# Two 64-wide attention layers: scores of two heads from 64-row array tiles, in periods of four PSUM banks

## The chip, the core and the metric

The kernel runs on one NeuronCore of a Trainium2 chip. Its engines run side by side and meet only at semaphores: TensorE (PE in the profile; its weight loads are PEld), VectorE (DVE), ScalarE (ACT), GpSimd (POOL) and SyncE (SP), which issues the large DMAs. TensorE writes to PSUM, eight banks of 128 partitions by 512 float32; DVE and ACT read PSUM. The metric is the device time of one execution in microseconds (us). Before the change it is 3609.78 us, the median of 3 runs (3605.16 to 3612.27).

## What is computed

Four layers are applied to 4 batches of 512 tokens of width 256, all in float32. The change touches the attention of the last two layers only, called L2 and L3 here. Cut to what matters:

```python
# L2: 16 heads of 64; one key and value head of 64 shared by all; 512 keys from the context
q = (xn @ Wq).reshape(b, n, 16, 64).transpose(0, 2, 1, 3) * 64 ** -0.5
k, v = kv[..., :64], kv[..., 64:]
attn = softmax(einsum('bhid,bjd->bhij', q, k)); out = einsum('bhij,bjd->bhid', attn, v)
# L3: 16 heads of 64, keys and values per head, 1024 keys (512 of them with a mask)
weight = einsum('bhld,bhnd->bhln', q, k) / 8
weight = softmax(where(full_mask, weight, -FLT_MAX)); out = einsum('bhln,bhnd->bhld', weight, v)
```

## The kernel before

The program is one instruction stream per engine with hand-placed semaphore waits. It goes through layer 0 attention, an expert layer, layer 1, and from about 1430 us through L2 and L3 once per batch: L2 of batch 0 alone, then a loop over three passes that each do L3 of batch b and L2 of batch b+1, then L3 of the last batch.

Both attentions come from one helper, `attention`, called as `att2` and `att3`. Its unit is a step: one head and 128 of the 512 queries. Two heads make a group, which has 4 query tiles x 2 heads = 8 steps; there are 8 groups, so 64 steps per call. `banks` is the number of PSUM banks that the scores of a step fill: 1 in L2 (512 keys), 2 in L3 (1024 keys). A step goes through these stations:

- `score` (L221, PE): one 512-column matmul per bank. The contraction is 64 long, but it is done over all 128 rows: the queries of both heads lie in `qT`, and each head has its own key tile `kH[..][s]` whose other 64 rows hold zeros. A float32 matmul is two passes of the array, two rows of the profile.
- `find` (DVE): the row minimum of the negated scores, L275 in L2; in L3 the mask is added in the same instruction, L277.
- `exponent` (L316, ACT): the exponential from PSUM to `probs` (the tile `pbuf`) with the row sum.
- `invert` and `divide` (L283 and L288, DVE): the reciprocal of the sum, and the probabilities times it.
- `turn` (L233, PE): four 128x128 transposes per bank into PSUM bank 4 or 5, in turns.
- `keep_turned` (L326, ACT): the copy of that bank to SBUF (`work`).
- `values` (L243, PE), once per group: probabilities times values, the two heads in the two 64-column halves of the array; `keep_values` (L292, DVE) copies the result.

Scores have banks 0 to 3 as a ring: `ring` = 4 steps in L2 and 2 in L3. PE runs ahead by that many steps, and DVE divides `behind` = 2 or 1 steps after it finds. PE's order in a step is `score(n + ring)`, `turn(n)`, and then at most a few jobs. Jobs are pieces of other work laid between the steps: the projections of the next group (L2: queries, L1692; L3: queries L1692, keys twice L1896, values twice L1904, each four 512-column or sixteen 128-column passes), and in the loop the normalisation of the next batch (during L3) or the last linear layer (during L2). PE makes a job's product in bank 7 and waits for DVE's copy of the one before (`jobs_kept`).

## Time and profile before

| what | us |
|---|---|
| median of 3 runs | 3609.78 |
| span of the profiled execution | 3697.7 |
| L2 attention, batch 0 alone | 128.20 |
| L2 attention in the loop, three calls | 131.98, 131.97, 131.98 |
| L3 attention in the loop, three calls | 297.11, 297.11, 297.13 |
| L3 attention, last batch alone | 289.85 |
| one pass of the loop (L2's last `values` of one to that of the next) | 554.99 |

The profiled execution has no time of its own beside its span, which is 88 us longer than the median of the runs. The eight attention calls, each counted from its first score matmul to the first matmul behind it, make up 1705 us of the span. Busy time is the sum of an engine's instructions; the end of a matmul is modelled, and consecutive ones overlap by their latency, so the distance between the starts of two matmuls tells what PE really needs for the first.

### The profile page before, as it was taken

Reading aid. Unit: us, or ns where it says so; the run is one execution under the profiler, and the core shown is the slowest. Engines: PE = TensorE matmul, PEld = TensorE weight load, DVE = VectorE, ACT = ScalarE, POOL = GpSimd, SP = SyncE. Lnnn points to the kernel's source line nnn. Section 1 sums busy time; section 2 is a strip of 40 time slices with the busy share of each in tenths; the row PEclk is TensorE's granted clock in tenths of the full one; section 3 lists DMA queues with packets and bytes.
Section 4 is the critical chain, followed back from the end, with each engine's and each line's share of the span. In section 5 each row is a group of like instructions: output and inputs, shape, how many; then the busy total and the mean of one; then the engine's idle time right before and its main releaser. Section 6 shows DMA issues by size and latency. Waiting matters only on the chain. (4 is left out here: it accounts for less than half of the span.)

```text
span 3697.7 us, 39640 instructions
## 1 busy us (share of the span) xinstructions
PE 3091.5 (84%) x13360; PEld 1710.1 (46%) x13360; DVE 2076.9 (56%) x5810; ACT 1450.9 (39%) x3056; POOL 384.7 (10%) x458
## 2 busy tenths in 40 slices
PE   7887877456077576998999988999988999988997
PEld 3443434222035254554555454555454555454554
DVE  6675756411357576634665734665734665734655
ACT  5463635221022221623444623444623444623443
POOL 0021202142652440000000000000000000000000
PEclk9998989678577777999999999999999999999998
DMA  1000000188562532001001001001001001001000
GB/s 47 15 13 15 12 15 12 60 252 243 101 83 29 85 46 86 1 3 67 1 1 46 1 19 57 1 1 46 1 18 58 1 1 46 1 19 45 1 1 6
DMA packets 47720, 143.61 MB, mean 39 GB/s; under 512 B 13735, under 2 KB 21287, under 8 KB 43563
## 3 DMA queue, kind: packets, MB, share of 16 engines
q1 hardware_dynamic: 32682, 111.82, 9.0%
q0 software_dynamic: 14848, 29.45, 5.9%
q8 instruction: 97, 1.59, 0.2%
q14 instruction: 93, 0.75, 0.1%
HBM read 128.43 MB, written 12.80 MB: 38 GB/s over the span
## 5 line engine op out<-in xcount | busy, mean ns | idle before, releaser
L221 PE MATMUL ps<-kH,qT 128*128 128x512 f32 x2048 | 1016.6, 601 | 26.3 <-issue 10.4
L326 ACT ACTIVATE work<-ps 128x512 f32<-128x512 f32 x768 | 430.3, 596 | 735.7 <-PE ps L233 466.7
L277 DVE CUSTOM_DVE_ANT_0 ps<-ps,mask 128x1024 f32<-128x1024 f32 x256 | 314.9, 1230 | 363.0 <-PE ps L221 361.1
L316 ACT ACTIVATE pbuf<-ps,least 128x512 f32<-128x512 f32 (+1 forms) x512 | 460.7, 900 | 132.6 <-DVE least L275 112.8
L233 PEld LDWEIGHTS ps<-consts,pbuf 128*128 128x128 f32 x3072 | 363.3, 141 | 279.6 <-issue 181.8
L221 PEld LDWEIGHTS ps<-kH,qT 128*128 128x128 f32 x2048 | 339.6, 192 | 269.0 <-issue 244.2
L233 PE MATMUL ps<-consts,pbuf 128*128 128x128 f32 x3072 | 421.1, 273 | 10.9 <-DVE pbuf L288 10.9
L243 PE MATMUL ps<-work,vh 128*64 128x512 f32 x1536 | 343.7, 596 | 5.7 <-ACT work L326 5.7
L288 DVE TENSOR_SCALAR pbuf<-pbuf,recip 128x512 f32<-128x512 f32 (+1 forms) x512 | 315.0, 615 | 10.9
L326 ACT ACTIVATE pt<-ps 128x512 f32<-128x512 f32 x256 | 152.4, 597 | 175.1 <-remote 84.6
L233 PEld LDWEIGHTS ps<-consts,probs 128*128 128x128 f32 x1024 | 124.6, 143 | 192.5 <-issue 106.9
L1233 POOL DMA_INDIRECT yg<-expert_rows,idx x192 | 201.0, 1047 | 91.5 <-issue 53.8
L243 PEld LDWEIGHTS ps<-work,vh 128*64 128x64 f32 x1536 | 104.5, 137 | 226.5 <-issue 218.9
L233 PE MATMUL ps<-consts,probs 128*128 128x128 f32 x1024 | 162.1, 281 | 40.6 <-issue 21.4
L489 POOL DMA_INDIRECT slot_token<-token_i,place x128 | 125.1, 977 | 639.3 <-DVE token_f L805 531.4
L316 ACT ACTIVATE probs<-ps,least 128x512 f32<-128x512 f32 x256 | 175.0, 683 | 37.8 <-DVE least L277 36.8
L277 DVE CUSTOM_DVE_ANT_0 ps<-ps,mask_add 128x512 f32<-128x512 f32 x256 | 174.3, 681 | 19.7 <-remote 11.6
L275 DVE TENSOR_REDUCE least<-ps 128x1 f32<-128x512 f32 x256 | 172.7, 675 | 13.1 <-PE ps L221 12.8
L283 DVE RECIPROCAL recip<-sums 128x1 f32<-128x1 f32 x768 | 121.8, 159 | 84.2 <-ACT probs L316 29.1
L1896 PE MATMUL ps<-arena 128*128 128x512 f32 x256 | 127.7, 623 | 27.2 <-ACT arena L1972 27.2
L1332 PE MATMUL ps<-ctxT,gw 128*36 128x512 f32 x32 | 23.0, 885 | 136.7 <-DMA ctxT<-in_ctxT 136.7
L1904 PE MATMUL ps<-arena 128*128 128x128 f32 x1024 | 127.6, 279 | 0.0
(288 smaller groups left out, 3645.6 us busy)
## 6 DMA issues: line engine op xcount, KB each, us to landing
wgu<-in_L_wgu SPq DMA_DIRECT2D x32, 768.0 KB
wd<-in_L_wd SPq DMA_DIRECT2D x32, 384.0 KB
arena<-in_L_wo SPq DMA_DIRECT2D x8, 1024.0 KB, 10.3
arena<-in_L_wff SPq DMA_DIRECT2D x4, 2048.0 KB, 9.4
ctxT<-in_ctxT SPq DMA_DIRECT2D x8, 512.0 KB, 3.7
expert_rows<-y SPq DMA_DIRECT2D x32, 128.0 KB
xb<-x_scratch SPq DMA_DIRECT2D x8, 512.0 KB, 3.5
ctxb<-in_ctx SPq DMA_DIRECT2D x8, 512.0 KB, 4.7
```

What stands on the lines that cost most here:

```text
L221: last = nc.tensor.matmul(scores(n)[:, kb * BANK:(kb + 1) * BANK], q_of(g, s, qt), k_of(g, s, kb), start=True, stop=True)
L233: last = nc.tensor.transpose(ps[:, 4 + m % 2, c * P:(c + 1) * P], probs[n % np_][:, kc * P:(kc + 1) * P], ident)
L243: last = nc.tensor.matmul(ps[rows * s:rows * (s + 1), 6, :], v_of(g, s, kc), pts[g % len(pts)][:, s, kc, :], start=kc == 0, stop=kc == nk - 1)
L275: nc.vector.tensor_reduce(least[:, n % 8:n % 8 + 1], x, AX.X, ALU.min).then_inc(least_ready, 1)
L277: nc.vector.tensor_tensor_reduce(out=x, in0=x, in1=mask, scale=1.0, scalar=FMAX, op0=add, op1=ALU.min, accum_out=least[:, n % 8:n % 8 + 1])\
L288: nc.vector.tensor_scalar(p, p, recip[:, n % 8:n % 8 + 1], None, mult).then_inc(probs_ready, 1)
L316: nc.scalar.activation(probs[n % np_], scores(n), ACT.Exp, bias=least[:, n % 8:n % 8 + 1], scale=-1.0, accum_out=sums[:, n % 8:n % 8 + 1]) ...
L326: nc.scalar.activation(pts[g % len(pts)][:, s, kb * 4:kb * 4 + 4, qt * P:(qt + 1) * P], ps[:, 4 + m % 2, :].rearrange("p (c q) -> p c q", ...
L489: nc.gpsimd.indirect_dma_start(taken_d[:, :], bass.IndirectOffsetOnAxis(place8[:, t, k:k + 1], 0), token_i[:, t:t + 1], None, bounds_check ...
L1233: nc.gpsimd.indirect_dma_start(yg[j % 2][:, k, :], None, y_d[:, :], bass.IndirectOffsetOnAxis(idx8s[u][:, t * TOPK + k:t * TOPK + k + 1], ...
L1896: last = nc.tensor.matmul(ps[:, bank, :], wkx[:, c, g * P:(g + 1) * P], keysT[:, c, kb * BANK:(kb + 1) * BANK], start=c == 0, stop=c == DC ...
L1904: last = nc.tensor.matmul(ps[:, bank, i * P:(i + 1) * P], keysT[:, c, tok], wvx[:, c, g * P:(g + 1) * P], start=c == 0, stop=c == DC - 1)
```

## The change

L2 and L3 use a new helper, `attention_pairs`; layer 0 keeps `attention`.

- Scores: the two heads of a group are two matmuls with a contraction of 64, one from rows 0 to 63 of `qT` and `kH`, one from rows 64 to 127. `kH` is one tile per buffer without zeros, and its copies (L1706 and L1915 in the helper jobs, L1935 for the first group) are one instruction, not two.
- The unit is a period: four score banks, which is U = 4 steps in L2 and 2 in L3. PE scores a whole period ahead, and only once all exponentials of the period before have been read from those four banks.
- `turn` goes in two halves of two banks each. Half 0 is copied to SBUF by DVE, half 1 by ACT. Both halves use banks 4 and 5, so half 1 waits for DVE's copies, and half 0 of the next period for ACT's.
- DVE makes one reciprocal per half; GpSimd makes the divisions.
- Jobs keep their step numbers, but are placed behind the half in which their step lies; DVE does its part at the end of a period.

```diff
--- before.py
+++ after.py
+def attention_pairs(nc, sem, name, ps, ident, groups, banks, q_of, k_of, v_of, mask, bufs, out, jobs):
...
+    U = 4 // banks
+    HALF = U // 2
+    nk = 4 * banks
+    per = 2 * NT
+    N = groups * per // U
+    each_group = per // U
+    probs, sums, recip, least, pts = bufs
...
+    def where(n):
+        g, r = divmod(n, per)
+        return g, r // 2, r % 2
...
+    def turned_at(p, half, j):
+        n = p * U + half * HALF + (j if banks == 1 else 0)
+        return n, (0 if banks == 1 else j)
+    def turned_to(p, half, j):
+        n, kb = turned_at(p, half, j)
+        g, qt, s = where(n)
+        return pts[g % len(pts)][:, s, kb * 4:kb * 4 + 4, qt * P:(qt + 1) * P]
+    def turned_from(j):
...
+        def score(p):
+            g = p // each_group
+            if p % each_group == 0 and need[g]:
+                pe.wait_ge(jobs_kept, need[g])
+            if p:
+                pe.wait_ge(exp_ready, p * U)
+            if banks == 1:
+                for n in range(p * U, (p + 1) * U):
+                    g, qt, s = where(n)
+                    nc.tensor.matmul(scores(n), q_of(g, s, qt), k_of(g, s, 0), start=True, stop=True).then_inc(scores_ready, 1)
+                return
+            for kb in range(banks):
+                for n in range(p * U, (p + 1) * U):
+                    g, qt, s = where(n)
+                    last = nc.tensor.matmul(scores(n)[:, kb * BANK:(kb + 1) * BANK], q_of(g, s, qt), k_of(g, s, kb),
+                                            start=True, stop=True)
+                    if kb == banks - 1:
+                        last.then_inc(scores_ready, 1)
+        def turn(p, half):
+            for j in range(2):
+                n, kb = turned_at(p, half, j)
+                if j == 0 or banks == 1:
+                    pe.wait_ge(probs_ready, n + 1)
+                if half:
+                    pe.wait_ge(kept_v, 2 * p + j + 1)
+                elif p:
+                    pe.wait_ge(kept_a, 2 * (p - 1) + j + 1)
+                for c in range(4):
+                    kc = kb * 4 + c
+                    last = nc.tensor.transpose(ps[:, 4 + j, c * P:(c + 1) * P], probs[n % np_][:, kc * P:(kc + 1) * P], ident)
+                last.then_inc(turned, 1)
+        def values(g):
+            pe.wait_ge(kept_v, 2 * each_group * (g + 1))
+            pe.wait_ge(kept_a, 2 * each_group * (g + 1))
+            if g:
+                pe.wait_ge(av_kept, g)
+            for kc in range(nk):
+                for s in range(2):
+                    last = nc.tensor.matmul(ps[64 * s:64 * (s + 1), 6, :], v_of(g, s, kc), pts[g % len(pts)][:, s, kc, :],
+                                            start=kc == 0, stop=kc == nk - 1)
+            last.then_inc(av_ready, 1)
+        score(0)
+        for p in range(N):
+            if p + 1 < N:
+                score(p + 1)
+            if p and p % each_group == 0:
+                values(p // each_group - 1)
+            for half, jobs_here in enumerate(halves(p, before)):
+                turn(p, half)
+                for job in jobs_here:
+                    project(job)
+        values(groups - 1)
...
+        def invert(p, half):
+            n = p * U + half * HALF
+            v.wait_ge(exp_ready, n + HALF)
+            at = slice(n % 8, n % 8 + HALF)
+            nc.vector.reciprocal(recip[:, at], sums[:, at]).then_inc(recip_ready, 1)
+        def keep_turned(p, j):
+            g = p // each_group
+            if p % each_group == 0 and g >= len(pts):
+                v.wait_ge(av_ready, g - len(pts) + 1)
+            v.wait_ge(turned, 4 * p + j + 1)
+            nc.vector.tensor_copy(turned_to(p, 0, j), turned_from(j)).then_inc(kept_v, 1)
+        def keep_values(g):
+            v.wait_ge(av_ready, g + 1)
+            nc.vector.tensor_copy(out[:, g, :], ps[:, 6, :]).then_inc(av_kept, 1)
+        for n in range(U):
+            find(n)
+        invert(0, 0)
+        invert(0, 1)
+        for p in range(N):
+            if p + 1 < N:
+                for n in range((p + 1) * U, (p + 2) * U):
+                    find(n)
+            if p and p % each_group == 0:
+                keep_values(p // each_group - 1)
+            for j in range(2):
+                keep_turned(p, j)
+                if p + 1 < N:
+                    invert(p + 1, j)
+            for jobs_here in halves(p, before):
+                for job in jobs_here:
+                    keep_job(job)
+        keep_values(groups - 1)
...
+        def exponent(n):
+            act.wait_ge(least_ready, n + 1)
+            if n >= np_:
+                act.wait_ge(turned, (n - np_ + 1) * banks)
+            nc.scalar.activation(probs[n % np_], scores(n), ACT.Exp, bias=least[:, n % 8:n % 8 + 1],
+                                 scale=-1.0, accum_out=sums[:, n % 8:n % 8 + 1]).then_inc(exp_ready, 1)
+        def keep_turned(p, j):
+            g = p // each_group
+            if p % each_group == 0 and g >= len(pts):
+                act.wait_ge(av_ready, g - len(pts) + 1)
+            act.wait_ge(turned, 4 * p + 2 + j + 1)
+            nc.scalar.activation(turned_to(p, 1, j), turned_from(j), ACT.Copy).then_inc(kept_a, 1)
+        for n in range(U):
+            exponent(n)
+        for p in range(N):
+            if p + 1 < N:
+                for n in range((p + 1) * U, (p + 2) * U):
+                    exponent(n)
+            for j in range(2):
+                keep_turned(p, j)
+    def divide(pool):
+        for n in range(groups * per):
+            pool.wait_ge(recip_ready, n // HALF + 1)
+            x = probs[n % np_]
+            nc.gpsimd.tensor_scalar(x, x, recip[:, n % 8:n % 8 + 1], None, mult).then_inc(probs_ready, 1)
...
-        kH = [[keep(f"kH_{i}{s}", [P, KEYS3]) for s in range(2)] for i in range(2)]
+        kH = [keep(f"kH_{i}", [P, KEYS3]) for i in range(2)]
...
-            def copy(v):
-                for s in range(2):
-                    r = slice(64 * s, 64 * s + 64)
-                    last = nc.vector.tensor_copy(kH[0][s][r, 0:S], ps[r, 7, :])
-                return last
-
-            return product, copy
+            return product, lambda v: nc.vector.tensor_copy(kH[0][:, 0:S], ps[:, 7, :])
...
-        att2 = attention(nc, sem, "a2", ps, ident, 2, HP, NT,
-                         lambda g, s, qt: qT[g % 2][:, qt * P:(qt + 1) * P],
-                         lambda g, s, kb: kH[0][s][:, 0:S],
-                         lambda g, s, kc: vh[0][:, kc, 0:DH2], DH2, None,
+        def head(s):
+            return slice(64 * s, 64 * s + 64)
+        att2 = attention_pairs(nc, sem, "a2", ps, ident, HP, 1,
+                         lambda g, s, qt: qT[g % 2][head(s), qt * P:(qt + 1) * P],
+                         lambda g, s, kb: kH[0][head(s), 0:S],
+                         lambda g, s, kc: vh[0][:, kc, 0:DH2], None,
...
-        att3 = attention(nc, sem, "a3", ps, ident, 2, HP, KEYS3 // P,
-                         lambda g, s, qt: qT[g % 2][:, qt * P:(qt + 1) * P],
-                         lambda g, s, kb: kH[g % 2][s][:, kb * BANK:(kb + 1) * BANK],
-                         lambda g, s, kc: vh[g % 2][:, kc, s * DH2:(s + 1) * DH2], DH2, mask3[:, :],
+        att3 = attention_pairs(nc, sem, "a3", ps, ident, HP, 2,
+                         lambda g, s, qt: qT[g % 2][head(s), qt * P:(qt + 1) * P],
+                         lambda g, s, kb: kH[g % 2][head(s), kb * BANK:(kb + 1) * BANK],
+                         lambda g, s, kc: vh[g % 2][:, kc, s * DH2:(s + 1) * DH2], mask3[:, :],
...
-                for i in range(2):
-                    nc.vector.memset(kH[i][0][64:P, :], 0.0)
-                    link(nc.vector.memset(kH[i][1][0:64, :], 0.0))
...
+            @block.gpsimd
+            def _(pool):
+                att3[6](pool)
+                att2[6](pool)
```

## Rows read from the trace of the kernel before

**Rows 1.** The page: the clock granted to PE, in 40 slices, in tenths.

```profile
PEclk9998989678577777999999999999999999999998
```

**Rows 2.** Windows: length, busy (instructions) of PE, PEld, DVE, ACT, POOL; clock; DMA.

```profile
1473.68:1601.88 128.20, 126.19 (x541) 62.76 (x541) 82.62 (x206) 82.27 (x193) 0.00 (x0) 1.00 0.00 1
3129.54:3261.52 131.98, 128.51 (x557) 64.14 (x557) 95.27 (x252) 82.38 (x193) 0.00 (x0) 1.00 0.09 37
3370.07:3659.92 289.85, 285.54 (x1333) 159.69 (x1333) 171.28 (x313) 141.57 (x257) 0.00 (x0) 1.00 0.00 1
```

**Rows 3.** Timeline of one L2 step: start, length in us, engine, line, operation.

```profile
3202.17 1.02 PE L221 MATMUL ps<-kH,qT 128*128 128x512 f32 x2
3202.45 0.67 DVE L275 TENSOR_REDUCE least<-ps 128x1 f32<-128x512 f32 x1
3203.04 0.48 DVE L288 TENSOR_SCALAR pbuf<-pbuf,recip 128x512 f32<-128x512 f32 x1
3203.46 1.02 PE L221 MATMUL ps<-kH,qT 128*128 128x512 f32 x2
```

**Rows 4.** Timeline around the values of two L2 groups, two groups apart.

```profile
3180.01 3.65 PE L243 MATMUL ps<-work,vh 128*64 128x512 f32 x16
...
3211.76 3.65 PE L243 MATMUL ps<-work,vh 128*64 128x512 f32 x16
...
3215.35 1.12 PE L221 MATMUL ps<-kH,qT 128*128 128x512 f32 x2
...
3216.51 0.69 DVE L275 TENSOR_REDUCE least<-ps 128x1 f32<-128x512 f32 x1 [0.28 <-PE ps L221]
```

**Rows 5.** Chain of waits through an L3 group: start us, us, what.

```profile
3401.96 1.72 PE ps L221 x4
3404.55 1.72 PE ps L221 x4
3406.27 0.87 PE ps L233 x8
...
3408.86 7.02 PE ps L243 x32
3415.88 1.91 PE ps L221 x4
...
3427.28 1.79 PE ps L1904 x16
...
3445.54 7.02 PE ps L243 x32
```

**Rows 6.** Timeline at the start of an L3 call, before the pipeline is full.

```profile
3373.56 1.11 ACT L316 ACTIVATE pbuf<-ps,least 128x1024 f32<-128x1024 f32 x1 [2.24 <-DVE least L277]
...
3374.82 1.98 PE L221 MATMUL ps<-kH,qT 128*128 128x512 f32 x4 [1.05 <-ACT pbuf L316]
...
3376.84 1.23 DVE L277 CUSTOM_DVE_ANT_0 ps<-ps,mask 128x1024 f32<-128x1024 f32 x1 [0.93 <-PE ps L221]
```

**Rows 7.** Timeline: a DVE copy of a PSUM bank and the instruction behind it.

```profile
3458.52 0.69 DVE L292 COPY wide<-ps 128x512 f32<-128x512 f32 x1
...
3459.13 1.22 DVE L277 CUSTOM_DVE_ANT_0 ps<-ps,mask 128x1024 f32<-128x1024 f32 x1
```

**Rows 8.** Groups of GpSimd instructions: busy, mean ns of one, idle before.

```profile
L1297 POOL TENSOR_SCALAR_AFFINE_SELECT eT<-eT 128x128 f32<-128x128 f32 x64 | 18.5, 307 | 34.7 <-ACT eT L1449 34.1
L971 POOL COPY column<-taken 128x1 uint32 x28 | 5.2, 184 | 46.7 <-PE ps L992 46.7
```

**Rows 9.** Timeline of PE in the expert layer, and of PE ahead of an L3 call.

```profile
857.67 1.51 PE L1001 MATMUL ps<-wgu,xgT 128*64 128x384 f32 x8 [0.47 <-DMA wgu<-in_L_wgu]
860.52 0.42 PE L1009 MATMUL ps<-consts,h 128*96 128x128 f32 x2 [1.34 <-DVE h L1100]
...
862.75 2.83 PE L1001 MATMUL ps<-wgu,xgT 128*64 128x384 f32 x8 [0.43 <-DMA wgu<-in_L_wgu]
...
3354.91 3.78 PE L1896 MATMUL ps<-arena 128*128 128x512 f32 x4 [5.46 <-ACT arena L1972]
```

More of the change, by code:

```diff
@@ L1912, in keys @@
             def keys(kb):
-                def copy(v):
-                    for s in range(2):
-                        r = slice(64 * s, 64 * s + 64)
-                        last = nc.vector.tensor_copy(kH[g % 2][s][r, kb * BANK:(kb + 1) * BANK], ps[r, 7, :])
-                    return last
-                return lambda pe: key_product(g, kb, 7), copy
+                return (lambda pe: key_product(g, kb, 7),
+                        lambda v: nc.vector.tensor_copy(kH[g % 2][:, kb * BANK:(kb + 1) * BANK], ps[:, 7, :]))
             def vals(kb):
@@ L1933, in keep_first @@
             if kind == "keys":
-                for s in range(2):
-                    r = slice(64 * s, 64 * s + 64)
-                    last = nc.scalar.activation(kH[0][s][r, kb * BANK:(kb + 1) * BANK], ps[r, bank, :], ACT.Copy)
-                return last
+                return nc.scalar.activation(kH[0][:, kb * BANK:(kb + 1) * BANK], ps[:, bank, :], ACT.Copy)
             if kind == "values":
@@ L2139, in _ @@
                 r2_vector(v)
+            @block.gpsimd
+            def _(pool):
+                att3[6](pool)
+                att2[6](pool)
         link.n = 0
@@ L2161, in _ @@
                 rest[1](v)
+            @block.gpsimd
+            def _(pool):
+                att3[6](pool)
 def kernel(**inputs):
```

60 lines of the change are left out of this document (added).

## Prediction

> **What bounds the kernel now.** The windows over the eight attention calls come first. PE is busy 126.2 of 128.2 us in L2 alone, 128.5 of 132.0 in L2 of the loop and 285.5 of 289.9 in L3, with the full clock; DVE is busy 59 to 72% of them, ACT 49 to 64%, GpSimd not at all [rows 2]. The timeline of a step then shows why. In L2 one step follows the next by 1.29 us [rows 3]: two score passes and four transposes. The chain of waits through an L3 group is all PE [rows 5]: four score passes take 1.72 us (0.43 each), eight transposes 0.87, together the 2.59 us between two steps. A group takes 31.75 / 2 = 15.88 us in L2 [rows 4] and 36.68 in L3 [rows 5]. So a cheaper score matmul is on the path, but only until something else is later.
>
> **Scores in pairs.** Of the 0.43 us per pass, half should go if two 64-row passes run at once. The nearest row is the value product, where two heads share the array by columns: 32 passes take 7.02 us, so 16 pairs at 0.43 and 0.14 over, and the next scores take 1.91 where 1.72 is usual [rows 5]. A pair thus costs as much as one pass, and going into such a mode and out again about 0.33. No row shows pairs by rows, so a pair costs between 0.43 (side by side) and 0.86 (one behind the other). I take 0.43, the row of the same array split the other way. Per L2 group 16 passes become 8 pairs, per L3 group 32 become 16: 3.4 and 6.9 us less PE work, over 4 x 8 groups of each 330 us. Off that go mode changes, some 0.2 us for each of the new ones. The Trainium skill, "TensorEngine Tiling (Array Packing)", section Tiling Modes, says that different tiles can compute in parallel, and that a change of mode drains the engine. The overhead of the value rows agrees with the second.
>
> **The period's loop.** Here the gain is lost. Before, PE was two or four steps ahead in a ring. Now the four banks are one buffer, and there is a second loop through banks 4 and 5. In iteration p PE issues `score(p+1)`, half 0, half 1. Half 1 waits for `kept_v`, DVE's copies of half 0, and these are queued on DVE behind all finds of p+1, which wait for the scores just issued. Only then can PE go on to `score(p+2)`. Counted from a period's first score:
>
> - L3: the finds can start at 2.02 (scores at 3374.82, L277 at 3376.84) [rows 6]. Two finds of 1.23 [rows 6] end at 4.48. Two copies of a bank: one starts 0.61 after the other and lasts 0.69 [rows 7], so 1.30. Then 0.05 for a semaphore, 0.10 for a weight load that is not hidden, 0.43 for four transposes and 0.10 to leave the mode: 2.02 + 2.46 + 1.30 + 0.68 = 6.46 us for two steps, which were 5.19. The exponentials are earlier: the second starts about 0.1 behind its find, and PE is free 1.26 after its start [rows 6], at 5.8.
> - L2: the finds start at 1.16 (L221 at 3215.35, L275 at 3216.51) [rows 4], four of 0.59 (start to start in [rows 3]): 1.16 + 2.36 + 1.30 + 0.68 = 5.50 us for four steps, which were 5.18.
>
> PE alone would need 1.72 + 1.74 + 0.3 = 3.8 us of either period. Only periods with the value product or with jobs are filled by PE.
>
> **Group by group.** L2 has two periods. The first holds scores 1.72, values 3.44, transposes 1.74, the query job 1.72 and four changes of mode at 0.15: 9.2. The second is the loop, 5.5. Sum 14.7, against 15.88. L3 has four. The first: scores 1.72, values 6.88, transposes 1.74, two jobs 3.44, changes 0.6: 14.4. In the second one job hides in half 0, but the value job in half 1 waits for DVE's copy of the one before, at 6.7, and adds 1.79 [rows 5]: 8.5. Third and fourth are loops, the one job hidden: 2 x 6.46. Sum 35.8, against 36.68. With 32 groups of each: -38 and -28 us. At the ends: a call begins with one period that nothing covers (5.2 us in L2, 5.9 in L3, where the ring needed 4 to 5), and its last group has no jobs to fill PE. Laid out per call, L2 is 5.2 + 2 x 5.5 + 6 x 14.7 + 15.4 = 119.8 against 128.2 [rows 2], and L3 is 5.9 + 29.9 + 6 x 35.8 + 36.0 = 286.6 against 289.85 [rows 2]. In the loop L3 has 7.3 us of normalisation jobs; some 3 of them hide in idle half 0. Sum: -4 x 8.4 - 4 x 3.3 - 3 x 3 = -56 us.
>
> **The clock.** PE was hardly idle in these calls, and the clock stayed full. In the fourth L3 period it now works some 3.4 of 6.46 us, with a pause of about 2.4 in one piece. The expert layer shows what that can do: there PE pauses 1.34 us behind 1.51 us of L1001, and the next eight of L1001 take 2.83 [rows 9], that is 1.2 GHz and not 2.4; the page has slices of 0.6 to 0.8 there [rows 1]. Behind a pause of 5.46 us four passes take 3.78 [rows 9] against 1.72. I expect one fall in two groups of three of L3, none in L2 (its longest pause is 1.5 us), and price it at 1.6 us, since the transposes and scores behind it, 2 us at full clock, nearly double: 32 x 2/3 x 1.6 = 34. Each of the eight calls also begins with a pause of 3 to 4 us: 8 x 1.5 = 12. Sum +46. Its bounds are 0 and, with two falls in every L3 group, +115. The Trainium skill, "TensorE: Matmul & The Clock Gate", section on the clock gate, has the same two levels and says that idling throttles the array; the rows of the expert layer agree.
>
> **GpSimd.** 256 divisions of 128x512 and 256 of 128x1024 leave DVE. The nearest rows are an instruction on 128x128 at 307 ns and a copy of one column at 184 [rows 8]. A 128x1024 one is then between 0.184 + 8 x 0.123 = 1.2 us and 8 x 0.307 = 2.5; I take 1.7, between them, since the fixed part is seen but not the rate of this operation. The reciprocal of half 0 is ready at about 5.2 of the period, and its transposes come at 6.46 + 2.0; half 1 has until 11.6 for both. So up to about 3.2 us each is hidden by PE's own scores, and GpSimd adds nothing to the sum. The Trainium skill, "GPSIMD Engine Reference", section 3.1, gives 1.8 cycles per element at 1.2 GHz at best, 1.5 us here, also hidden. No run here shows it.
>
> **Small edits.** One key copy where there were two takes some 0.7 us [rows 7] per L3 key job off DVE, each behind a PE product that is later; four memsets lie under the first loads. Both nothing, at most -5.
>
> **Sum.** -56 + 46 = -10 us against the profiled execution, 3697.7 to 3688. The 88 us between it and the median are not located; I carry the difference over unchanged: 3610 - 10 = 3600.
>
> **Rivals.** (A) The forecast, 3600, its own range 3580 to 3620. (B) The clock holds, because the pauses are split by transposes: -56, 3554. For it: the longest pause is half that ahead of L3. Against: the expert layer falls behind a shorter one. (C) The loop is longer than its rows: waits that no row shows, at PE's two waits or at DVE's copies, or further falls. Some 112 periods are bound by the loop (32 in L2, 80 in L3); at 0.5 us each +56, so 3656, slower. It decides from 0.1 us each. For it: every station now waits for another one in turn, and each hop is shown only once. (D) The change does not do what it says: row pairs run one behind the other. Each period's scores take 1.72 us more, at the head of the loop: 4 x 32 + 4 x 16 = 192 periods, +330 less the clock loss that then goes: about 3880. For it: two 128-column results go to PSUM at once, which no row shows. GpSimd above 3.2 us, for which no row speaks, would look like C.
>
> **Chances.** A 0.42, B 0.27, C 0.23, D 0.08. A measurement of this kernel tells 0.2% (7 us) from no change. Of A half lies below 3603, a quarter within. Faster: B and most of half of A, 0.49; same: 0.12; slower: C, D and the rest of A, 0.39. The range leaves out D and the ends of B and C: 3535 to 3680.
>
> **What would show it.** Right: in L2 and L3 the score passes start in pairs, 0.43 apart; in L3 periods without values or jobs PE waits some 2.4 us for DVE's `keep_turned`, and the period is 6.4 to 6.6 us; DVE's copies sit directly behind the finds; GpSimd ends before PE asks. Groups of 14.7 and 35.8 us plus the clock. The granted clock below 1 in L3 only. Wrong: PE waiting for GpSimd or for ACT's exponentials at the head of a period, score passes 0.86 apart, or groups over 16 and 37.5 us at full clock.

## The result and the profile after

The changed kernel takes 3658.19 us (median of 4 runs, 3655.99 to 3659.97), the kernel before in the same visit 3607.47 us: ratio 1.0144, 95% interval 1.0130 to 1.0159. It is 51 us slower. The forecast was 3600, 10 us faster. The time lies inside the range, near rival C (3656), but that is luck: C's main mechanism, longer loops, is not what the trace shows. The ratios here and below leave out one execution of run e12, the profiled one, which ran at a lower granted clock throughout (4136.77 us, the others 3604.68 to 3621.44).

Windows over three of the eight attention calls, the changed kernel (L2 alone, L2 in the loop, L3 last; columns as in [rows 2], which they answer):

```profile
1374.84:1503.76 128.92, 112.03 (x541) 53.71 (x541) 71.35 (x142) 64.44 (x161) 98.84 (x64) 0.94 0.00 1
...
3065.61:3202.65 137.04, 116.84 (x556) 56.73 (x557) 88.86 (x188) 64.39 (x161) 100.12 (x64) 0.93 0.09 35
...
3310.50:3616.97 306.47, 270.09 (x1332) 139.78 (x1332) 151.41 (x299) 115.14 (x193) 181.18 (x64) 0.93 0.00 1
```

PE has 14 us less busy time in L2 alone and the call is 0.7 us longer; in the last L3 call 15 us less busy time and 16.6 us longer. The clock, the third figure from the right, is the news: 0.93 and 0.94 where every call of before had 1.00.

The measure used below, "the calls", is a sum of five spans that hold the eight calls: L2 alone, three stretches of the loop from L3's first score pass to the end of L2's last value product, and the last L3 call. Each stretch also holds 15.5 us of other work between its two calls, the same in every kernel, so the sum stands 46.6 us above the eight calls by themselves (1702.4 before, 1756.4 after); the expectations call it the sum of the eight calls. It is 1749.0 us before and 1803.0 after: +54.0, which is the whole difference. (The rest of the program took 1852 us in the profile of after, and 1947 to 1958 or 1851 to 1859 in the profiles further down, by the visit and not by the kernel. The profile of before had 1949 there; that is where its surplus over the median lies. So absolute times are not compared across visits, ratios and the calls are.)

PE's timeline through a steady L3 group (start, length in us; L428 scores, L454 values, L444 transposes, L1912, L2113 and L2121 jobs), which answers [rows 5]:

```profile
3430.73 3.17 PE L454 MATMUL ps<-work,vh 128*64 128x512 f32 x14
...
3439.35 1.99 PE L428 MATMUL ps<-kH,qT 64*128 64x512 f32 x8
...
3447.90 1.99 PE L428 MATMUL ps<-kH,qT 64*128 64x512 f32 x8
...
3454.47 1.99 PE L428 MATMUL ps<-kH,qT 64*128 64x512 f32 x8 [0.16 <-DVE vh L2135]
3456.39 1.09 PE L444 MATMUL ps<-consts,pbuf 128*128 128x128 f32 x8
3459.64 1.23 PE L444 MATMUL ps<-consts,pbuf 128*128 128x128 f32 x8 [2.17 <-DVE work L503]
3460.80 3.28 PE L428 MATMUL ps<-kH,qT 64*128 64x512 f32 x8
3464.01 7.44 PE L454 MATMUL ps<-work,vh 128*64 128x512 f32 x32
```

To see here: eight passes of 64 rows take 1.99 us, the time of four of 128 rows, so they do run in pairs. The periods are 8.55, 6.57 and 6.33 us. In the last one PE stands 2.17 us before half 1, for DVE's copy of half 0 (L503). Right behind that pause the same eight passes take 3.28 us instead of 1.99, and the value product that follows 7.44 where 7.09 is usual. In the L3 calls of the loop the fall comes a little earlier: the value product is at 7.09, but the transposes before the scores take 1.5 to 1.7 us instead of 1.23, and the scores 3.0 to 3.3. Each of the six steady groups of each L3 call has one stretch at half clock, 24 in all, and the kernel before has none in any call; steady groups are 37.4 to 37.65 us, against 36.68 before. The window over these scores alone:

```profile
3460.80:3464.01 3.21, 3.21 (x10) 0.96 (x9) 0.00 (x0) 0.70 (x2) 3.21 (x2) 0.59 0.02 5
```

The end of the last L3 call, PE's and GpSimd's rows. There is no next score to cover anything:

```profile
3591.96 1.23 PE L444 MATMUL ps<-consts,pbuf 128*128 128x128 f32 x8 [2.17 <-DVE work L503]
3593.12 1.99 PE L428 MATMUL ps<-kH,qT 64*128 64x512 f32 x8
...
3598.32 5.66 POOL L556 TENSOR_SCALAR pbuf<-pbuf,recip 128x1024 f32<-128x1024 f32 x2 [0.67 <-DVE recip L496]
...
3601.21 1.93 PE L444 MATMUL ps<-consts,pbuf 128*128 128x128 f32 x8 [1.69 <-POOL pbuf L556]
...
3604.03 1.97 PE L444 MATMUL ps<-consts,pbuf 128*128 128x128 f32 x8 [0.89 <-POOL pbuf L556]
...
3606.73 9.46 PE L454 MATMUL ps<-work,vh 128*64 128x512 f32 x32 [0.73 <-issue]
```

The two divisions take 2.83 us each, PE waits for both, and the last value product takes 9.46 us where 7.09 is its full-clock time. The first two rows hold a warning: here a pause of 2.17 us stands before the transposes too, and the scores behind it keep 1.99 us; so do those of the first group in two of the loop's L3 calls. So the length of one pause does not decide by itself whether the clock falls. L2's call ends in the same way, on four divisions of 1.55 us:

```profile
1493.38 0.66 PE L444 MATMUL ps<-consts,pbuf 128*128 128x128 f32 x4 [0.88 <-POOL pbuf L556]
...
1494.92 0.81 PE L444 MATMUL ps<-consts,pbuf 128*128 128x128 f32 x4 [0.88 <-POOL pbuf L556]
...
1498.30 5.52 PE L454 MATMUL ps<-work,vh 128*64 128x512 f32 x16 [0.73 <-issue]
```

GpSimd by form (busy us, mean ns | idle before), which answers the guess made from [rows 8]:

```profile
L556 POOL TENSOR_SCALAR pbuf<-pbuf,recip 128x1024 f32<-128x1024 f32 x256 | 725.0, 2843 | 922.1 <-DVE recip L496 922.1
L556 POOL TENSOR_SCALAR pbuf<-pbuf,recip 128x512 f32<-128x512 f32 x256 | 399.2, 1576 | 301.9 <-DVE recip L496 301.9
```

### The profile page after: what moved, and what is told of

It is laid out like the page before. It is cut to its first block and busy times, and to the rows that moved or that the text cites. A ratio compares the mean times of both kernels' runs of the same rounds, so it can differ in the third digit from the quotient of the medians.

```text
span 3654.7 us, 39585 instructions
## 1 busy us (share of the span) xinstructions
PE 2921.7 (80%) x13360; PEld 1587.1 (43%) x13360; DVE 1978.3 (54%) x5490; ACT 1264.3 (35%) x2664; POOL 1509.7 (41%) x970
## 5 line engine op out<-in xcount | busy, mean ns | idle before, releaser
L556 POOL TENSOR_SCALAR pbuf<-pbuf,recip 128x512 f32<-128x512 f32 (+1 forms) x512 | 1124.1, 2210 | 1224.0 <-DVE recip L496 1224.0
L444 PE MATMUL ps<-consts,pbuf 128*128 128x128 f32 x3072 | 456.4, 288 | 161.6 <-DVE work L503 144.2
L444 PEld LDWEIGHTS ps<-consts,pbuf 128*128 128x128 f32 x3072 | 342.8, 144 | 412.1 <-POOL pbuf L556 200.4
L454 PE MATMUL ps<-work,vh 128*64 128x512 f32 x1536 | 358.9, 618 | 6.0 <-issue 6.0
L541 ACT ACTIVATE work<-ps 128x512 f32<-128x512 f32 x384 | 223.4, 596 | 379.9 <-PE ps L444 368.9
L428 PE MATMUL ps<-kH,qT 64*128 64x512 f32 x1024 | 290.9, 692 | 23.0 <-ACT pbuf L533 15.8
L221 PE MATMUL ps<-kH,qT 128*128 128x512 f32 x512 | 261.8, 598 | 6.3 <-DVE qT L908 5.6
L503 DVE COPY work<-ps 128x512 f32<-128x512 f32 x384 | 258.2, 679 | 8.5 <-PE ps L444 8.4
L454 PEld LDWEIGHTS ps<-work,vh 128*64 128x64 f32 x1536 | 110.4, 142 | 253.0 <-issue 253.0
L507 DVE COPY wide<-ps 128x512 f32<-128x512 f32 x64 | 44.3, 692 | 262.2 <-PE ps L454 262.2
L428 PEld LDWEIGHTS ps<-kH,qT 64*128 64x128 f32 x1024 | 100.9, 212 | 141.8 <-issue 104.6
L2113 PE MATMUL ps<-arena 128*128 128x512 f32 x256 | 131.0, 636 | 28.2 <-ACT arena L2181 27.5
```

The costliest lines, as they stand in the source:

```text
L221: last = nc.tensor.matmul(scores(n)[:, kb * BANK:(kb + 1) * BANK], q_of(g, s, qt), k_of(g, s, kb), start=True, stop=True)
L428: last = nc.tensor.matmul(scores(n)[:, kb * BANK:(kb + 1) * BANK], q_of(g, s, qt), k_of(g, s, kb), start=True, stop=True)
L444: last = nc.tensor.transpose(ps[:, 4 + j, c * P:(c + 1) * P], probs[n % np_][:, kc * P:(kc + 1) * P], ident)
L454: last = nc.tensor.matmul(ps[64 * s:64 * (s + 1), 6, :], v_of(g, s, kc), pts[g % len(pts)][:, s, kc, :], start=kc == 0, stop=kc == nk - 1)
L503: nc.vector.tensor_copy(turned_to(p, 0, j), turned_from(j)).then_inc(kept_v, 1)
L541: nc.scalar.activation(turned_to(p, 1, j), turned_from(j), ACT.Copy).then_inc(kept_a, 1)
```

## The experiments

Three theories are tried. K: the half clock behind PE's pauses is the loss. G: GpSimd's slow divisions are, where nothing covers them. L: the chain of waits through the four banks is, whatever the clock does. Every run is compared with the kernel before in the same visit.

| kernel | ratio to before (95%) | the calls, us | steady group L3 / L2 |
|---|---|---|---|
| before | 1 | 1749.0 | 36.7 / 15.88 |
| changed | 1.0144 (1.0130 to 1.0159) | 1803.0 | 37.5 / 14.72 |
| e1 | 1.0074 (1.0057 to 1.0091) | 1777.3 | 36.8 / 15.51 |
| e2 | 1.0283 (1.0265 to 1.0302) | 1846.5 | 36.8 / 15.51 |
| e3 | 1.0183 (1.0162 to 1.0204) | 1814.6 | 37.5 / 15 to 16.5 |
| e4 | 1.0552 (1.0534 to 1.0569) | 1946.4 | 40.4 / 17.0 |
| e5 | 0.9955 (0.9939 to 0.9971) | 1744.2 | 35.9 / 14.72 |
| e6 | 0.9879 (0.9853 to 0.9904) | 1702.7 | 33.8 / 14.72 |
| e7 | 0.9795 (0.9774 to 0.9816) | 1664.3 | 33.8 / 13.94 |
| e8 | 0.9741 (0.9721 to 0.9762) | 1651.5 | 33.8 / 13.95 |
| e9 | 0.9731 (0.9700 to 0.9763) | 1659.5 | 33.8 / 13.95 |
| e10 | 0.9707 (0.9682 to 0.9733) | 1645.1 | 33.8 / 13.95 |
| e11 | 1.0323 (1.0298 to 1.0347) | 1868.8 | 38.2 / 16.74 |
| e12 | 1.0023 (1.0008 to 1.0037) | not read | not read |

### e1, e2, e5 and e12: more work in the pause

If the clock is the cause, giving PE something useless to do in the pause must make the kernel faster.

```
         for half, jobs_here in enumerate(halves(p, before)):
             turn(p, half)
+            if half == 0 and not any(job[0] is not None for job in jobs_here):
+                fill(4 if banks == 2 else 3)
...
+        def fill(times, bank=7):
+            if bank == 7 and done[0]:
+                pe.wait_ge(jobs_kept, done[0])
+            for _ in range(times):
+                nc.tensor.matmul(ps[:, bank, :], ident, spare, start=True, stop=True)
```

> The changed kernel, plus matmuls whose result nobody reads: wherever half 0 of a period has no job, PE writes bank 7 four times (L3) or three times (L2) before it asks for the copies that half 1 waits for. Theory K (the half clock behind PE's pause of 2.17 us is the loss): the scores behind a jobless L3 period go back from 3.28 to 1.99 us and the value products from 7.45 to 7.09, so a steady L3 group falls from 37.55 to 35.8 us. About 30 such groups: -50 us, 3608, ratio to the kernel before 0.997 to 1.003, although PE does more. L2 groups stay at 14.7. Theory G (GpSimd's 2.83 us per division, waited for at starts and ends of calls) and theory L (the chain of waits itself, whatever the clock): the groups stay at 37.5, 3655 to 3665, since the added matmuls hide in the pause at best.

Measured: ratio 1.0074, calls 1777.3, half of what K expected. L3 groups fell to 36.82 and L2 groups rose to 15.51. The trace shows that the fault is in the dose. A matmul of this kind is two passes of 0.43 us, not one, so four of them take 3.44 us in a pause of 2.17 (L462 is the fill):

```profile
3526.10 1.99 PE L428 MATMUL ps<-kH,qT 64*128 64x512 f32 x8 [0.16 <-DVE vh L2143]
...
3528.95 3.60 PE L462 MATMUL ps<-consts 128*128 128x512 f32 x8
3532.39 1.04 PE L444 MATMUL ps<-consts,pbuf 128*128 128x128 f32 x8
3533.35 1.99 PE L428 MATMUL ps<-kH,qT 64*128 64x512 f32 x8
3535.27 7.09 PE L454 MATMUL ps<-work,vh 128*64 128x512 f32 x32
```

The scores behind it are back at 1.99 and the values at 7.09: the clock held, and the period, 7.25 us, is now filled by PE's own work. The second run had the same fault in more places.

```
         score(0)
+        fill(8, 6)
...
+                if p == N - 1:
+                    fill(2 if half else 4)
                 turn(p, half)
...
+        fill(2)
         values(groups - 1)
```

> As the one before, and also eight unread matmuls behind the first scores of each call (bank 6), and 4, 2 and 2 of them ahead of the last three waits of each call (two halves of the last period, last value product). Theory K: the second scores of a call fall from 3.78 to 1.99, the last value product from 9.46 to 7.1 (L3) and from 5.52 to 3.65 (L2): some 4 us in each of 8 calls more than the run before, -80 us in all, 3575 to 3585, ratio 0.99 to 0.993: faster than the kernel before. Theory G: the waits for GpSimd at the ends stay, and nothing is gained but what the first run gained. Rival within K: matmuls ahead of a wait that is short (0.7 us) make PE late themselves, +0.5 us per call.

Measured: 1846.5. The steady groups are those of e1. The first scores of the last L3 call lie 8.99 us before the second, which were 5.93 apart, and from the last but one value product to the last it takes 38.9 us where it took 30.09 in the changed kernel. This is twice the intended work, in places without cover, and as a forecast of the time the expectation is a miss. What it says of the clock came true: in seven of the eight calls no stretch is at half clock, the second scores take 1.99 us, and the last value products 7.09 and 3.65. The clock was kept, at a price above what it is worth.

So the dose was fitted, with the changed kernel as the base again:

```
+                    fill(2 if banks == 2 else 1)
```

> As the first run (unread matmuls in jobless half 0), but two of them (1.72 us) in L3 and one (0.86 us) in L2, so that they fit into pauses of 2.17 and 1.38 us; the first run's four and three took 3.44 and 2.58 and made the periods longer (7.25 where 6.34). The measure is the sum of the eight attention calls (first score to end of last value product), since the layers ahead take 1850 or 1950 us from one visit to the other: 1749.0 in the kernel before, 1803.0 in the changed one, 1777.3 in the first run. Theory K: steady L3 group 35.9 us (predicted working without a clock loss: 35.8), L2 14.7, calls 1725 to 1735: faster than the kernel before by 15 to 25 us, ratio 0.993 to 0.997. Rival: two matmuls leave 0.45 us of pause and PE's clock falls all the same, 37.0 to 37.5 per group, 1790 to 1803.

Measured: 0.9955 (0.9939 to 0.9971), calls 1744.2, L3 group 35.90, L2 group 14.72. A group of the last L3 call:

```profile
3501.93 1.99 PE L428 MATMUL ps<-kH,qT 64*128 64x512 f32 x8 [0.16 <-DVE vh L2143]
3503.85 1.09 PE L444 MATMUL ps<-consts,pbuf 128*128 128x128 f32 x8
3504.78 1.88 PE L462 MATMUL ps<-consts 128*128 128x512 f32 x4
3507.11 1.22 PE L444 MATMUL ps<-consts,pbuf 128*128 128x128 f32 x8 [0.45 <-DVE work L511]
3508.26 1.99 PE L428 MATMUL ps<-kH,qT 64*128 64x512 f32 x8
3510.18 7.09 PE L454 MATMUL ps<-work,vh 128*64 128x512 f32 x32
```

The period is still 6.33 us, the loop of waits untouched, with 1.72 us more work in it. Yet the group is 1.6 us shorter, 1.3 in the scores and 0.35 in the values. No steady L3 group has a stretch at half clock any more. That is K, by itself 1803.0 - 1744.2 = 59 us, more than the whole slowdown; 41 of it lie in the L3 calls and 18 in L2's, whose first and sixth groups in the loop and last value products had lost the clock too. L and G expected no change. (The profiled execution took 10 us more than the median of its kernel, so 59 is rather low than high; the ratio stands for 16 us under the kernel before.)

e5 does not hold the clock everywhere. Its last L3 call, from which the group above is taken, is at 0.98:

```profile
3362.89:3656.99 294.10, 274.50 (x1377) 143.95 (x1377) 151.43 (x299) 114.97 (x193) 181.39 (x64) 0.98 0.00 1
```

```
+                    fill(1 if banks == 2 else 0)
```

> The changed kernel with one unread matmul (0.86 us) in the jobless half 0 of L3, none in L2: half of what filled the pause before. The pause of 2.17 us is then 1.3 in one piece. Theory K in its simple form (a pause of that length costs nothing: L2's steady groups have one of 1.38 and stay at full clock): L3 group 35.9 as with two. Rival: what counts is how much PE works around the pause, not its length, and it still falls once a group: 37.0 to 37.5. L2 as in the changed kernel. Calls 1750 to 1760 by the first, 1790 to 1803 by the second.

Measured: 1.0023 (1.0008 to 1.0037), that is 7 us over the kernel before, so calls of about 1756. No group is read from its trace. The total fits the first reading, 1750 to 1760: in L3 half the dose does nearly all of it. That is shown by the total alone.

### e3 and e9: where the division is done

```
+        def split(p, half):
+            v.wait_ge(recip_ready, 2 * p + half + 1)
+            for n in range(p * U + half * HALF, p * U + (half + 1) * HALF):
+                x = probs[n % np_]
+                nc.vector.tensor_scalar(x, x, recip[:, n % 8:n % 8 + 1], None, mult).then_inc(probs_ready, 1)
...
             for job in jobs_here:
                 keep_job(job)
+            if p + 1 < N:
+                split(p + 1, half)
```

> The changed kernel with the divisions of a half on DVE, behind its copies and the jobs of that half, and nothing on GpSimd. Theory G: at the end of a call PE waits 2.6 us (L3) and 3.7 us (L2) for GpSimd, and in L2's start another 0.8 to 1.2 per period; with DVE's 0.5 to 0.9 us per division most of that goes, so 2 to 4 us per call, -15 to -30 us, 3628 to 3643, with steady groups as they were (14.7 and 37.5). Theory K: the same small gain at the ends, since the clock is not touched. Rival: DVE now has finds 2.46, copies 1.30, divisions 1.8 and reciprocals 0.3 in a period of 6.34, and a job's copy on top makes it the bound: L3 periods with one job grow by 0.2 to 0.5, 0 to +30 us in all.

Measured: 1.0183, calls 1814.6, 12 us more than the changed kernel, where 15 to 30 less were expected. G is right on two places. In L2 alone the way from the last but one value product to the end of the last falls from 18.8 to 14.0 us. The last L3 call is 6.7 us shorter (299.0 from its first score, was 305.7): 4.2 at its end, with the last value product at 7.09, and 2.5 at its start, where this run lost less to the clock (second scores 2.53 us, were 3.78). In the three L3 calls of the loop nothing is gained at the end, 38.6 us where 38.5 was: there the products for the next L2 call lie between the last transposes. The steady L3 group stays at 37.54, so GpSimd was hidden there. The rival showed in L2 and not in L3, where I had put it. On DVE a division of 128x1024 takes 0.744 us; L2 in the loop has DVE busy 111.2 of 144.1 us with it (88.9 of 137.0 without; the window below stops 2.8 us short, in the last value product). Its groups go from 15 to 17 and 19 us, and it has five stretches at half clock in its middle where the changed kernel has two:

```profile
3177.19:3318.50 141.31, 116.18 (x544) 58.49 (x546) 111.22 (x252) 64.18 (x161) 0.00 (x0) 0.90 0.09 34
```

So the division is better on DVE at the end of L3 and on GpSimd in L2's steady groups. The run e9 prices that in the version e8 below, by taking back only this edit:

> The version of the last run with L3's divisions on GpSimd again: it parts that run's two edits. Calls were 1664.3 with the jobs spread and 1651.5 with unread matmuls and DVE's divisions on top. Theory G: at the end of an L3 call PE waits for GpSimd (1.69 and 0.89 us in the changed kernel), so this one is 2 to 4 us longer per L3 call than the last: 1660 to 1668, and the unread matmuls alone bring little. Theory K: what was gained is the clock at the ends, brought by the unread matmuls: 1651 to 1655.

Measured: calls 1659.5, 8 us over e8, as G expected, but not for G's reason in each call. In the last L3 call it is: the way from the last but one value product to the last is 29.76 us with GpSimd and 28.09 without. The L3 calls of the loop are 0.4, 2.6 and 2.5 us longer; there 2.3 us more in the last group is also what e5 and e6, both with GpSimd, show in one of their three calls and not in the others, with the clock down in it. So 1.7 us is shown for GpSimd, and the rest of the 8 is open. The ratios, 0.9731 and 0.9741 in two visits, can't tell the two apart.

### e4 and e11: what the pairs are worth

```
-        kH = [keep(f"kH_{i}", [P, KEYS3]) for i in range(2)]
+        kH = [[keep(f"kH_{i}{s}", [P, KEYS3]) for s in range(2)] for i in range(2)]
...
-                         lambda g, s, qt: qT[g % 2][head(s), qt * P:(qt + 1) * P],
-                         lambda g, s, kb: kH[g % 2][head(s), kb * BANK:(kb + 1) * BANK],
+                         lambda g, s, qt: qT[g % 2][:, qt * P:(qt + 1) * P],
+                         lambda g, s, kb: kH[g % 2][s][:, kb * BANK:(kb + 1) * BANK],
```

> The changed kernel with keys padded to 128 rows, as in the kernel before, so that no two score passes run at once; periods, copies and GpSimd stay. If pairs save what the rows say, an L2 period issues 1.72 us of passes where it had 0.86 x 2 ... that is 4 x 0.43 against 2 x 0.43, and L3 3.44 against 1.72. L2 group: the period bound by PE grows by 0.86, the loop does not: 15.6 us. L3 group: first period 14.4 + 1.7, second +1.4, two loops 7.7 each where they were 6.4: about 41.5 plus the clock's loss, which stays (PE still pauses 2.6 us for DVE's copies). Sum +0.9 x 32 + 4.5 x 32 = +170 us, 3800 to 3850, ratio 1.05 to 1.07. If pairs do not run at once, no change: 3658. That gives the price of the periods alone against the kernel before.

Measured: 1.0552, calls 1946.4. Without pairs the same structure is 143 us slower than with them; against the kernel before, the periods (with GpSimd's division) cost 197 us. The L3 group, 40.4, is near what was expected (41.5), but the clock's loss, which was to stay, is gone: no L3 call has a stretch at half clock between its first and its last but one value product. The pause is 1.47 us where 2.17 was, and 3.44 us of scores stand around it where 1.72 did. So the 143 us are the pairs' saving less what they cost in clock. The L2 group, 17.0, is not (15.6): I had counted one pass where a score has two, so that both periods pay 1.72 us or some less:

```profile
1541.54 3.70 PE L423 MATMUL ps<-kH,qT 128*128 128x512 f32 x8
1545.07 1.04 PE L444 MATMUL ps<-consts,pbuf 128*128 128x128 f32 x8
1546.71 1.28 PE L444 MATMUL ps<-consts,pbuf 128*128 128x128 f32 x8 [0.60 <-DVE work L503]
1547.83 3.60 PE L423 MATMUL ps<-kH,qT 128*128 128x512 f32 x8
```

The fourth period of an L3 group, with the shorter pause and the scores behind it at full speed:

```profile
3653.05 1.22 PE L444 MATMUL ps<-consts,pbuf 128*128 128x128 f32 x8 [1.47 <-DVE work L503]
3654.11 3.60 PE L428 MATMUL ps<-kH,qT 128*128 128x512 f32 x8
```

e11 is the same edit on e8:

> The best version with padded keys, so that no two score passes run at once: what do the pairs bring where jobs are spread and the clock holds? Rows of the fourth run: scores take 3.44 us of a period, not 1.72. L2 group: 13.95 + 2 x 1.72 = 17.4, less what of the loop PE then hides. L3 group: first period +1.72, three loop periods: second half's copies end at 3.0 + 2.46 + 1.3 = 6.8, +0.7 = 7.5 where 6.4 is, together 33.75 + 1.7 + 3.3 = 38.8. Calls: 1651 + 32 x 3.0 + 32 x 5.0 = about 1900, ratio 1.03 to 1.05 to the kernel before: the pairs carry the whole gain. Rival: the order of jobs and the held clock carry it, and pairs are worth less than half of the 98 us: 1750 or less.

Measured: 1.0323, calls 1868.8, groups 38.17 and 16.74. In the version where the clock mostly holds, the pairs are worth 217 us, and without them all other improvements together don't reach the kernel before. The 74 us between 217 and 143 are near what the pairs cost the changed kernel in clock; no run separates that from the other changes in e8.

### e6, e7, e8 and e10: real work in the pause

Useless matmuls show a cause. Better is to move jobs out of the period that PE fills anyway into those where it waits.

```
-            return [q_job(wqx, latT, g), keys(0), keys(1), vals(0), vals(1)]
+            own = {0: q_job(wqx, latT, g), 1: vals(0), 2: keys(0), 4: keys(1), 6: vals(1)}
+            return own
...
-                         jobs=jobs3)
+                         jobs=lambda g, i: ([jobs3(g + 1)[i]], i == 4) if g + 1 < HP and i in (0, 1, 2, 4, 6) else ([], False))
```

> The changed kernel with the five jobs of an L3 group at steps 0, 1, 2, 4 and 6 instead of 0 to 4 (queries, values 0, keys 0, keys 1, values 1), so that each of the three loop periods has one job in half 0 and none has two or none. Nothing is added. Theory K plus L: a job of 1.72 us in half 0 is hidden by the wait for DVE's copies, and fills the pause: period 6.57 each with the clock full; group 14.3 + 3 x 6.57 = 34.0 us where 37.5 was; 28 such groups: -98 us, calls 1700 to 1715, ratio to the kernel before 0.985 to 0.99. If only the order of the jobs counted and the clock still fell once a group: 35.7, 1750. If jobs in the loop lengthened it (DVE's copy of the job ahead of the next finds): +0.3 us per period, 34.9.

Measured: 0.9879, calls 1702.7, steady L3 group 33.75 to 33.87 (expected 34.0). Nothing is added or left out, only the order of five jobs differs, and it is 100 us. Of a group's 3.7 us, 1.6 are the clock (e5). The rest fits the half 1 that had held a second job of a loop period, 8.55 us, and has none now.

```
-                         jobs=lambda g: [q_job(wq2, xnT2, g)])
+                         jobs=lambda g, i: ([q_job(wq2, xnT2, 1)], True) if (g, i) == (0, 0) else
+                         ([q_job(wq2, xnT2, g + 2)], True) if i == 4 and g + 2 < HP else ([], False))
```

> As the run before, and in L2 the query job of group g+2 in the second period of group g (half 0) instead of that of g+1 in its first period. Theory L: the first period loses 1.72 us, the second has a pause of 1.38 us in half 0 that a job of 1.72 fills, and grows by 0.35 plus a copy of 0.67 on DVE that nothing waits for: L2 group 7.5 + 5.9 = 13.4 us where 14.7 was, 28 such groups: -36 us, calls about 1670 and ratio 0.97 if the run before gives 1705. Rival G: GpSimd needs 8 x 1.55 = 12.4 us for the divisions of an L2 group and each of them begins late, so GpSimd becomes the bound: 14.0 to 14.5.

Measured: 0.9795, calls 1664.3, L3 group as in e6, L2 group 13.94. The sum is as expected, the group half a microsecond longer than L's 13.4; what it lacks came from the first groups in the loop, 14.18 us where e6 had 17.4 to 17.7. It is not G: PE waits for DVE's copy, 0.51 us in the period that now has no job between its halves. The second period, 1519.86 to 1525.48, is 5.62 us with the job in it:

```profile
1519.86 1.99 PE L424 MATMUL ps<-kH,qT 64*128 64x512 f32 x8
1521.78 1.09 PE L445 MATMUL ps<-consts,pbuf 128*128 128x128 f32 x8
1522.71 1.88 PE L1913 MATMUL ps<-xnT,wq 128*128 128x512 f32 x4
1524.43 1.12 PE L445 MATMUL ps<-consts,pbuf 128*128 128x128 f32 x8
1525.48 1.99 PE L424 MATMUL ps<-kH,qT 64*128 64x512 f32 x8
1527.40 3.65 PE L455 MATMUL ps<-work,vh 128*64 128x512 f32 x16
1530.99 1.09 PE L445 MATMUL ps<-consts,pbuf 128*128 128x128 f32 x8
1532.59 1.29 PE L445 MATMUL ps<-consts,pbuf 128*128 128x128 f32 x8 [0.51 <-DVE work L504]
```

e8 adds the fill of e5 and, in L3, the `split` of e3:

> As the run before, with the fitted unread matmuls in halves that still have no job (last group of a call, L2's start), and the divisions of L3 back on DVE (L2's stay on GpSimd). Theory K and G: the last value products at full clock (7.1 and 3.65) and no wait for GpSimd at L3's end, some 5 us per L3 call and 2 per L2 call: -25 to -30 us from the run before. Rival: DVE now has 2.46 + 1.30 + 0.3 + 1.8 and a job's copy 0.67 = 6.5 us of work in a period of 6.57, so L3 periods with a job become DVE's: +0.2 to 0.5 us each, 96 of them, +20 to +50.

Measured: 0.9741, calls 1651.5, 13 us less than e7, half of what was hoped. The rival did not come: L3 groups stay at 33.75. The last value products are at 7.09 in all L3 calls, but still at 5.35 us in two of L2's four.

e10 adds a fill at the start of each call:

```
         score(0)
+        fill(4 if banks == 2 else 2, 6)
```

> The best version so far, and behind the first scores of each call four (L3) or two (L2) unread matmuls in bank 6, 3.44 and 1.72 us in pauses of 3.94 and 2.26. Theory K: the second scores of a call go from 3.78 back to 1.99 us in the calls where they are at half clock: up to 1.3 to 1.8 us in each of 8 calls, calls 1638 to 1650. Rival: PE is already at half clock when the call begins, since the layer ahead leaves it idle, so the unread matmuls themselves take twice their time (6.9 us in a pause of 3.9) and delay the second scores: 1655 to 1675.

Measured: 0.9707 (0.9682 to 0.9733), calls 1645.1, the lowest. It beats the kernel before by 2.9%. Its interval overlaps that of e8; what tells the two apart is the trace, 6 us in the calls. The start of the last L3 call in e8 and in e10:

```profile
3287.14 1.99 PE L429 MATMUL ps<-kH,qT 64*128 64x512 f32 x8 [0.69 <-ACT vh L2169]
3293.07 3.78 PE L429 MATMUL ps<-kH,qT 64*128 64x512 f32 x8 [3.94 <-ACT pbuf L552]
```

```profile
3183.60 1.99 PE L429 MATMUL ps<-kH,qT 64*128 64x512 f32 x8 [0.69 <-ACT vh L2170]
3185.52 3.70 PE L463 MATMUL ps<-consts 128*128 128x512 f32 x8
3189.53 1.99 PE L429 MATMUL ps<-kH,qT 64*128 64x512 f32 x8 [0.31 <-ACT pbuf L553]
```

The second scores still come 5.93 us behind the first, but take 1.99 and not 3.78. The fill takes 3.70 us, so the rival, a fill at half clock, is out here. The window over this call shows the clock whole again, with PE busy less than before and the call 16 us shorter than in [rows 2]:

```profile
3183.60:3457.74 274.14, 260.34 (x1357) 138.68 (x1357) 193.22 (x363) 115.02 (x193) 0.00 (x0) 1.00 0.00 1
```

## Why the prediction was wrong, point by point

**Scores in pairs: right.** A pair costs one pass, 1.99 us for eight where four were meant to be paid; unpaired, in e4, eight take 3.70. Rival D is out. Its price was too high as well: e4, which is D by hand, costs 143 us more than the changed kernel and not some 280, since loops that wait for DVE hide part of the passes and the clock's loss goes.

**The loop: right.** 6.33 to 6.57 us in L3 periods with one job or none (6.46 forecast), 8.55 with two (8.5), and a pause of 2.17 us for `keep_turned` (2.4).

**Steady groups: right.** L2 14.72 (14.7). L3 with the clock held, in e5, 35.90 (35.8).

**The clock: right in kind, and the first of two terms that failed by size.** I took one fall in two of three L3 groups at 1.6 us, and 12 us at the starts: +46. It falls in each steady L3 group, and there 1.6 us is the right price (1.3 in the scores and 0.35 in the values in the last call). "None in L2" holds in most steady groups only. In the loop L2 loses the clock in its first and sixth group (17.4 and 19.4 us where e5 has a 15.7 and a 17.9), and the last value product takes 5.52 us for 3.65 in L2 alone, 6.45 in the loop, and 9.46 for 7.09 in the last L3 call; none of this was priced. e5 gives 59 us for what its fills reach. It still loses some 19 us, an estimate from its own rows: the second scores of calls take 2.46 to 3.78 us for 1.99, three L2 groups of the loop are 1.7 us above their like, one value product is 1.7 and one L3 end 2.3 us too long. Taken off, the three stretches of the loop, which differ by up to 6.5 us in e5, all come to 436.7 us, which speaks for the estimate. So the clock costs about 78 us where the sum had 46.

**The ends of the calls: the step of the work term that failed.** "Laid out per call, L2 is 119.8 and L3 286.6" took first and last group at little more than the loop's length. e5 has 126.7 and 293.3. Of these 7 us over each, 3.1 and 1.8 are still the clock at the start, and some 1.5 in L3 are the fills themselves, which are not covered in the last group (estimates from the same rows). What is left in L2 is mostly its end: from the last but one value product on it takes 16.5 us in e5, all at full clock, where the forecast leaves 13.7, and 14.0 in e3, which has no divisions on GpSimd. It is four divisions of 1.55 us to a period, 6.2 us of GpSimd against 5.5 of loop. In L3 it is the tail. Of the 36.0 us for the last group, 11.7 were left between the last scores and the last values (36.0 less 6.88, 6.46 and a first period of 14.4 without its two jobs). In the changed kernel they are 13.6: the scores start at 3593.12, the last transposes wait for two divisions in a row, which end at about 3601.15 and 3603.98, and the values start at 3606.73. I had called GpSimd hidden because steady groups hide it. e3 took it away: 4.9 us off the end of L2 alone and 4.2 off the end of the last L3 call, the clock's part of 1.9 and 2.4 us included.

**GpSimd's price: outside its bounds.** 2.84 us against 1.2 to 2.5, taken 1.7. I had scaled a 128x128 instruction of another operation. It stayed under the 3.2 us of cover, so the steady groups did not notice. The Trainium skill, "GPSIMD Engine Reference", section 3.1, gives 1.8 cycles per element as the best case, 1.5 us here by estimate; the trace has nearly twice that for this operation.

**The calls of the loop.** Each pair of L3 and L2 in the loop was to take 443.9 - 14.7 = 429.2 us without the clock's loss; e5 has 438.2 to 444.7, and 436.7 once its remaining falls are taken off. Half of these 7.5 us is what L2 alone shows too. The rest I can only argue: the background jobs (normalisation in L3, the linear layer in L2) fall into halves that wait for DVE, and L2's groups in the loop show 15.09, 15.29 and 17.9 us where L2 alone has 14.72. No run separates them. The ends of the loop's L3 calls are not it, by e3.

**The sum.** Forecast -56 + 46 = -10. Measured in the calls: +54. With the clock at about +78, the work is about -24. So of the 64 us of error about half, 32, lies in the clock and half in the work term: 4 and 5 us in the two calls that stand alone, and 3 x 7.5 in the loop. Without the estimate, from e5 alone, it would be +59 and -5; e5's ratio, 16 us under the kernel before, lies between the two. Rival C had the size for a wrong reason: "at 0.5 us each" for 112 loop periods, where the L3 periods came out within 0.13 us. Its "further falls" were the true half of it. The chances were also added wrongly: C, D and the quarter of A above make 0.415, not 0.39. The fault of the method was to spend the care on the steady group and to let each of eight starts and ends go at a rounded figure, in work and in clock; the prices carried over the steady groups were right within 0.1 us.

## What to carry to other kernels

When a change takes work off the busiest engine and adds a wait to it, ask what happens to TensorE's clock behind the wait, and put independent work of about its length into it; here that alone turned +1.4% into -0.5%. Ordering the real jobs by where PE waits made it -2.0% (e7), and fills and L3's divisions on DVE on top -2.9% (e10). Price the first and the last group of each call by their own chain, with no cover: a slow engine that is hidden in the steady state can be on the path there. And count how many passes one matmul call is before dosing a filler.

## What the runs showed of the hardware

- Two score passes of 64 rows at different row halves of the array run at once in 32-bit floats: x8 in 1.99 us, with the results in different PSUM banks.
- Around a pause of 2.17 to 2.28 us with little work beside it the granted clock fell to half, and the next scores took 3.0 to 3.3 us for 1.99, once in each of the 24 steady L3 groups. Behind pauses of 1.38 us in L2's steady groups it did not fall, nor behind 1.47 in L3 with unpaired scores (e4), nor behind 0.45 (e5). The pause alone does not decide: in the last group of the last L3 call, and in the first of two others, the same 2.17 us left the next scores at 1.99. With 0.86 us of work in the long one most of the loss was gone (e12, by its total only).
- The cheaper scores cost clock here: with 1.72 us more of score passes in each period (e4) the steady L3 groups kept the full clock, and their pause was 1.47 us.
- GpSimd divides 128x1024 by a column in 2.84 us and 128x512 in 1.58; DVE takes 0.744 for the former (e3).
- Adding 1.72 us of matmuls to a period made the group 1.6 us shorter (e5).
